# Moving four row copies ahead of V's second half in the first body, with a total and two signs later

## What is computed

```python
Q = (h @ Wq.T + bq)          # h = layernorm(x); 16 heads of 32; V likewise
latent = latent_keys.reshape(64, 16, 32)
logits = einsum('bhtd,lhd->bhtl', Q, latent) / sqrt(32)
w, idx = softmax of the 4 largest logits of each row
attn = (sum of w * latent[idx] + V) @ Wo.T + bo
x = x + layernorm(attn)
wu, wg, wd = ternary(W_up), ternary(W_gate), ternary(W_down)
    # scale = mean(|W|) + 1e-8; clip(round(W / scale), -1, 1) * scale
hidden = silu(layernorm(x) @ wu.T) * (layernorm(x) @ wg.T)   # 2048 wide
x = x + layernorm(hidden @ wd.T)
```

## Time and profile before

| what | value |
|---|---|
| median of 3 runs | 1028.66 us (1027.9 to 1029.03) |
| time of the profiled execution | 1029.43 us |
| its span | 1027.6 us |
| mean granted TensorE clock | 0.984 of full speed |
| PE busy | 966.2 us, 94% of the span |
| DVE, ACT, POOL busy | 71%, 50%, 52% |

### The profile page before, as it was taken

The page is one execution under the profiler, slowest core; times in us unless marked ns, Lnnn a source line. Parts: engine busy times, 40 slices in busy tenths (PEclk is TensorE's granted clock), DMA queues, the critical chain, the costliest instruction groups (busy, mean ns, idle before and its releaser), DMA issues.

```text
span 1027.6 us, 17907 instructions
## 1 busy us (share of the span) xinstructions
PE 966.2 (94%) x5738; PEld 469.4 (46%) x5738; DVE 729.3 (71%) x2666; ACT 513.9 (50%) x801; POOL 533.6 (52%) x451
## 2 busy tenths in 40 slices
PE   3738999999999999999999999999999999999997
PEld 2413544345444544445444454445444454445443
DVE  7898798376893689665993779836895669845433
ACT  5787986445534555345444455345453454433430
POOL 2556266645566446554666546564565545643330
PEclk9868999999999999999999999999999999999999
DMA  9953403532124402233113321243022511212001
GB/s 296 400 108 69 149 1 83 141 73 76 22 42 109 107 11 41 62 92 93 21 34 89 75 69 21 47 116 92 11 41 62 97 37 21 42 41 63 1 1 41
DMA packets 149331, 76.91 MB, mean 75 GB/s; under 512 B 135825, under 2 KB 135825, under 8 KB 148113
## 3 DMA queue, kind: packets, MB, share of 16 engines
q1 hardware_dynamic: 149264, 76.18, 29.5%
HBM read 34.21 MB, written 8.39 MB: 41 GB/s over the span
## 4 chain that ended last, share of the span: by engine, by line
PE 68%; DVE 15%; ACT 5%; POOL 5%; issue 4%; DMA 3%; SPq 0%; DVEq 0%; ACTq 0%; POOLq 0%
PE ug L709 36%; PE ug L728 14%; PE ring L559 10%; PE ring L687 4%; PE ring L605 2%; DVE Lr L1580 2%; DMA X1T<-halves 1%; DMA x_in<-in_x 1%; DVE v L1554 1%; DVE halves L1534 1%; DVE row L1671 1%; POOL halves L1297 1%; DVE sty L1674 1%; DVE stx L1694 1%; DVE ugt L1539 1%
## 5 line engine op out<-in xcount | busy, mean ns | idle before, releaser
L709 PE MATMUL ug<-X1T,TU 128*128 128x512 f16 (+1 forms) x1152 | 245.1, 356 | 6.3 <-DVE ugt L1544 4.2
L1274 POOL TENSOR_TENSOR hT<-ugt,hT 128x512 f16<-128x512 f32 x128 | 166.8, 1303 | 161.1 <-ACT hT L1026 161.1
L709 PE MATMUL ug<-X1T,TG 128*128 128x512 f16 (+1 forms) x1152 | 244.8, 355 | 0.0
L728 PE MATMUL ug<-TD,hT 128*128 128x512 f16 x960 | 210.9, 379 | 0.9 <-ACT TD L905 0.9
L1013 ACT ACTIVATE ugt<-ug,cu 128x512 f32<-128x512 f32 x128 | 87.9, 687 | 203.1 <-PE ug L709 202.2
L709 PEld LDWEIGHTS ug<-X1T,TU 128*128 128x128 f16 x1152 | 110.0, 98 | 116.2 <-DVE ugt L1544 4.9
L709 PEld LDWEIGHTS ug<-X1T,TG 128*128 128x128 f16 x1152 | 112.7, 98 | 108.6
L1539 DVE SCALAR_TENSOR_TENSOR ugt<-ugt,ug 128x512 f32<-128x512 f32 x128 | 87.4, 683 | 99.6 <-ACT ugt L1013 98.3
L728 PEld LDWEIGHTS ug<-TD,hT 128*128 128x128 f16 x960 | 93.2, 98 | 115.8 <-issue 3.0
L1580 DVE MATCH_REPLACE8 Lr<-v,Lb 128x68 f32<-128x68 f32 x512 | 102.3, 218 | 0.0
L1544 DVE SCALAR_TENSOR_TENSOR ugt<-ugt,ug 128x512 f32<-128x512 f32 x128 | 87.9, 687 | 4.4
(11 more groups left out here) (218 smaller groups left out, 1498.5 us busy)
## 6 DMA issues: line engine op xcount, KB each, us to landing
out_dram<-Lr SPq DMA_DIRECT2D x32, 256.0 KB, 3.2
x_in<-in_x SPq DMA_DIRECT2D x7, 1024.0 KB, 5.3
x<-in_x SPq DMA_DIRECT2D x28, 256.0 KB, 3.3
PT<-in_Wd SPq DMA_DIRECT2D x8, 512.0 KB, 6.7
hT<-in_Wu SPq DMA_DIRECT2D x4, 512.0 KB, 8.7
hT<-in_Wg SPq DMA_DIRECT2D x4, 512.0 KB, 15.4
x_in<-in_Wd SPq DMA_DIRECT2D x4, 512.0 KB, 5.1
x_in<-in_x SPq DMA_DIRECT2D x4, 256.0 KB, 4.3
```

What stands on the lines that cost most here:

```text
L709: last = pe.matmul(ug[:, 2 * (e % 2) + s, cols], w[:, k, e * P:(e + 1) * P], X1T[:, b, k, cols], start=(k == 0 and b == 0), stop=(k == KD ...
L728: last = pe.matmul(down_bank(kind, t), hT[:, a, e, t * P:(t + 1) * P], td[:, e, :], start=(first and e == of[0] and a == 0), stop=(final a ...
L1274: pool.tensor_tensor(hT[:, 1, e, :], ugt[:, 2 + e % 2, :], hT[:, 0, e, :], ALU.subtract).then_inc(h_lo, 1)
```

## The change

In the first body, ACT copies all four tiles of chunk 1's rows ahead of `vw_half(m, 1)`, and sums pieces 10 and 11 behind them. POOL makes chunk 1's row factors (`ln1_rstd_of(1)`) after two of the four first-half remainders, and all four `s1_lo` ahead of the second-half remainders. DVE makes `ln1_biases(1)` and Wo's remainder (`weights_lo(2)`) ahead of the total of the first matrix and the sum of piece 14; at the end, `t2_lo(0, 3)` ahead of `round_to(1)`. PE takes the gate matrix's total after `q(0)` of the second body. On ACT, `t2_rows(-1, 3)` comes ahead of `q(1)`. In the second body's loop the signs of pieces 7 and 15 move from block 6 to blocks 8 and 9. The order of DVE's roundings stays as it was, written out as `ROUND_ORDER`.

```diff
@@ -271,14 +271,15 @@
 
         ASUM_DVE = (2, 3, 14, 15)
         ASUM_ACT = (0, 1, 16, 17, 18, 19) + tuple(range(4, 14)) + tuple(range(20, 24))
-        TERN_ORDER = (0, 8, 1, 9, 4, 12, 2, 10, 5, 13, 3, 11, 6, 14, 7, 15, 22, 23, 16, 17, 20, 21, 18, 19)
+        TERN_ORDER = (0, 8, 1, 9, 4, 12, 2, 10, 5, 13, 3, 11, 6, 14, 22, 7, 15, 23, 16, 17, 20, 21, 18, 19)
 
         ROUND_ACT = (18, 19)
         ROUND_POOL = (0,)
+        ROUND_ORDER = (8, 1, 9, 4, 12, 2, 10, 5, 13, 3, 11, 6, 14, 7, 15, 22, 23, 16, 17, 20, 21)
 
         def rounded_before(n):
 
-            return sum(q not in ROUND_POOL for q in TERN_ORDER[:TERN_ORDER.index(n) + 1])
+            return ROUND_ORDER.index(n) + 1
 
         def after_tern(*pieces):
 
@@ -755,12 +756,13 @@
                     wo(2)
                     pe.wait_ge(tern_step, 1)
                     wo(3)
-                    wait(pe, a32_ready, i, KD, KD)
-                    total(weight_sum(1), tot[:, 1:2], tot_ready, 2, tota_ready)
                     return
                 if att:
                     for m in range(KD):
                         q(m)
+                        if kind == "second" and m == 0:
+                            wait(pe, a32_ready, j, KD, KD)
+                            total(weight_sum(1), tot[:, 1:2], tot_ready, 2, tota_ready)
                 logits_after = (8, 12) if kind == "second" else (6, 10)
                 for half in range(2):
                     upgate(0, half)
@@ -1080,16 +1082,16 @@
                     probs_hi(3)
                     vw_half(2, 0)
                     vw_half(3, 0)
-                    abs_sum(10)
-                    abs_sum(11)
                     s1_rows(1, 0)
                     s1_rows(1, 1)
+                    s1_rows(1, 2)
+                    s1_rows(1, 3)
                     vw_half(0, 1)
                     vw_half(1, 1)
                     vw_half(2, 1)
                     vw_half(3, 1)
-                    s1_rows(1, 2)
-                    s1_rows(1, 3)
+                    abs_sum(10)
+                    abs_sum(11)
                     abs_sum(12)
                     abs_sum(13)
                     t2_rows(0, 0)
@@ -1100,8 +1102,8 @@
                 if kind == "second":
                     q(0)
                     t2_rows(-1, 2)
+                    t2_rows(-1, 3)
                     q(1)
-                    t2_rows(-1, 3)
                     sign(1)
                     sign(9)
                     q(2)
@@ -1115,7 +1117,7 @@
                         if m < 2:
                             t2_rows(-1, 2 + m)
                 late = kind == "second"
-                SIGN_AT = {0: (2,), 1: (10,), 2: (5, 13), 3: (3, 11), 4: (6,), 5: (14,), 6: (7, 15), 8: (22,), 9: (23,), 10: (16,), 11: (17,), 12: (20,), 13: (21,)}
+                SIGN_AT = {0: (2,), 1: (10,), 2: (5, 13), 3: (3, 11), 4: (6,), 5: (14,), 8: (22, 7), 9: (15, 23), 10: (16,), 11: (17,), 12: (20,), 13: (21,)}
                 SUM_AT = {2: (4,), 3: (5,), 4: (6, 7)}
                 exp4_at = (4, 7, 12) if late else (3, 6, 11, 15)
                 exps_at = (6, 10, 15) if late else (5, 9, 13)
@@ -1318,17 +1320,17 @@
                     shift(3)
                     normalise(2)
                     normalise(3)
-                    for m in range(KD):
-                        low_a_half(m, 0)
+                    low_a_half(0, 0)
+                    low_a_half(1, 0)
                     ln1_rstd_of(1)
-                    s1_lo(1, 0)
-                    s1_lo(1, 1)
+                    low_a_half(2, 0)
+                    low_a_half(3, 0)
+                    for t in range(TT):
+                        s1_lo(1, t)
                     for m in range(KD):
                         low_a_half(m, 1)
                     rstd_y(0)
                     rstd_y(1)
-                    s1_lo(1, 2)
-                    s1_lo(1, 3)
                     rstd_x(0, 0)
                     rstd_y(2)
                     round_to(0)
@@ -1764,10 +1766,10 @@
                     probs_lo(2)
                     ln1_stat(1)
                     probs_lo(3)
+                    ln1_biases(1)
+                    weights_lo(2)
                     tern_total(0)
                     abs_sum(14)
-                    ln1_biases(1)
-                    weights_lo(2)
                     abs_sum(15)
                     y_a(0)
                     y_a(1)
@@ -1788,8 +1790,8 @@
                     y_b(3)
                     t2_lo(0, 2)
                     y_c(0, 3)
+                    t2_lo(0, 3)
                     round_to(1)
-                    t2_lo(0, 3)
                     round_to(9)
                     round_to(4)
                     round_to(12)
```

## The result

The changed kernel takes 1031.37 us (median of 10 runs, 1029.33 to 1032.67) against 1029.05 for the kernel before (10 runs beside it). The ratio is 1.0020, 95% interval 1.0011 to 1.0028: 1.1 to 2.9 us slower, best estimate 2.1. I had forecast 0.6 us faster.

A forecast was written before the change was run, and what follows sets the result against it. PE, busy 94% of the span, was taken to set the time after the opening; ACT's queue, then DVE's, orders blocks 0 to 7. A 0.6 gain at the first tanh carries through: 1028.66 - 0.6 = 1028.06, say 1028.0; range 1025.9 to 1029.8.

The forecast's parts named there:

- The gap of PE: PE between wo(3) and q(0): earlier rows fill XT sooner, so q ends at 97.5 instead of 104.08, 6.6 us sooner.
- The second idle stretch before X1T: PE after q: idles 2.8 us from 97.5, possibly at low clock for the first half blocks, which still end by about 107.
- DVE: DVE before y_a(0): factor about 1.2 sooner gains up to 1.0; 0.2 (0 to 0.5) taken for the y_a, y_b, y_c chain.
- What the rows push back: V's second half on ACT, its POOL remainders and wo(2) slightly later; 0.1 taken for wo(3), between 0 and 0.5.
- The end of the opening: ACT from t2_rows(-1, 3) to the first tanh: tanh at 109.75 in place of 110.34, a gain of 0.6.
- The 0.45 for the fourth rows: ACT's t2_rows(-1, 3) ahead of q(1): can begin at about 100.1 instead of 100.54, 0.45 sooner.
- The signs and the port: Second body's loop: moved signs cost nothing, with 0.15 to spare; DVE roundings meeting POOL taken as nothing, from -1.2 to +1.0.
- rival B: ACT in block 10: sign 15 delays the tanh beyond its cover, +1.04 and +0.2 against -0.6; 1029.3, chance 0.15.
- The prediction's term for the rounding at 151: DVE rounding beside POOL's probs_lo: 1.2 less if it goes first, 1.0 more if it waits; nothing taken.
- rival A: Port meeting falls well (-1.2) and PE's further waits shrink by up to 1.1, about -2.9 in all; 1025.8, chance 0.18.
- Rival C: PE's idling from 97.5 keeps half clock through all four half blocks, block 2 ending 2.1 later; 1030.8, chance 0.06.

The follow-up runs named there:

- e1: Kernel before with only POOL's row factor moved between the second and third of the four first-half remainders; ratio 1.0013 to the kernel before.
- e2: Changed kernel with POOL's row factor back behind all four first-half remainders; ratio 1.0017 to the kernel before.
- e10: Kernel before with POOL's row factor ahead of all four first-half remainders; ratio 1.0023 to the kernel before.
- e6: Changed kernel with DVE's total and sum of piece 14 back ahead of ln1_biases(1) and Wo's remainder; ratio 1.0017 to the kernel before.
- e15: Changed kernel with only the extra PE matmuls of e9 in both gaps, before and inside wo_first(0); ratio 1.0016 to the kernel before.
- e9: Kernel before with the factor early as in e1, ten unused PE matmuls before wo_first(0) and nine inside it; ratio 0.9996 to the kernel before.
- e13: Changed kernel with e6's edit and the extra PE matmuls of e9 in both gaps; ratio 1.0011 to the kernel before.
- e5: Kernel before with only t2_rows(-1, 3) ahead of q(1) on ACT and t2_lo(0, 3) ahead of round_to(1) on DVE; ratio 1.0002 to the kernel before.
- e4: Kernel before with only the signs of pieces 7 and 15 moved from block 6 to blocks 8 and 9; ratio 1.0005 to the kernel before.
- e7: e1 with ten extra matmuls on PE, product unread, between weigh_half(0) and wo_first(0); ratio 1.0006 to the kernel before.

## Why the prediction was wrong

**The gap of PE: right.** q ran from 88.6 to 99.2 at full clock, 1.5 later than forecast against the weigh half, since `wo(3)` ended late; XT was full in time, the total behind `q(0)` cost 0.14. (In the text, "4.7 of them the gap less the total" is the gap alone; less the total it is 4.4, and with the clock's 2.2 that is the 6.6.) The second idle stretch before X1T was there (2.96 at 102.20, I had said 2.8) and brought the low clock back for the first half blocks (0.60 granted on average from 102.2 to 106), covered by the transfer of tiles 2 and 3, as I had written. None of it reached the sum, as forecast.

**DVE: this is the step that failed.** I wrote that the factor "comes about 1.2 sooner, so DVE gains up to 1.0", and took 0.2 of gain. Against the weigh half the factor did come 1.2 sooner, but partly by luck: the power instruction started 2.2 sooner, met DVE's subtraction and took 1.0 more [e1; not in e2 or e10]. And `y_a(0)` came 1.72 later. The sum is -1.24 for the factor, +0.46 for the biases, +1.39 for Wo's remainder and +1.11 for the sum of piece 14 with its total. Two of these were in no part of the step. The sum of piece 14 had filled all but 1.00 of DVE's wait for the factor and was moved behind it, so it now lies on the path: e6 takes it back and gains 0.8 in `y_a(0)`. And Wo's remainder takes 5.02 instead of 3.64. It is four instructions, of 0.74 each where POOL is quiet. Before and in e2 only the fourth met a row subtraction of POOL and took 1.66 and 1.64; POOL's rows began 1.7 to 1.8 after Wo's remainder did in all three kernels, so their start alone is not the cause. In the changed kernel the early factor lets Wo's remainder start while POOL still has the delayed remainders of V; the first instruction takes 1.23 for that, so the third has not begun when POOL's rows do, and the third and the fourth take 1.64 each. It takes both moves: with the factor alone (e1) the rows begin 2.6 after it and it is 3.22, with the rows but the factor back (e2) it is 3.63. e15 shows that DVE's path alone holds `y_a(0)` at 16.3.

**What the rows push back: mis-sized.** I took 0.1 "between 0 and 0.5" for V's late second half. V's second remainders began at 81.81 where I had 80.2, since ACT's rows began at 74.79 and not at 73.19. The prediction contradicts itself there: it starts the rows at 73.19 and has the factor, which they need, only 1.2 sooner than 75.1. The term in front of `wo(2)`, the delay of the first-half remainders by the factor, I had not priced at all: 1.31 us of wait, and 3.4 us more at the low clock (71.6 to 79.0, for 71.35 to 75.3 before). It costs 1.04 in `y_a(0)` alone (e1), and by way of the clock: at full clock the same late remainder leaves `y_a(0)` at 14.31 (e9). In the changed kernel it is covered by DVE's longer path (e15). With both mended (e13), `y_a(0)` is still 0.6 late and the first tanh 1.2: DVE's slower remainder of Wo, and V's late second half by way of `wo(2)` and POOL's factor of y.

**The end of the opening: wrong, small.** The 0.45 for the fourth rows did not come. Measured from `y_c(0, 3)`, the first tanh is 10.39 behind it after and 10.30 before; in e5 it is 10.38. The rows start 0.26 sooner where I had 0.45, and the waits for roundings are 0.67 (0.27 and 0.40) where I had put 0.2 for both; together these are 0.7, the distance from the 0.6 forecast to the 0.09 lost. ACT's work in between, 9.5, was as forecast.

**The signs and the port: small gains.** From the first tanh to V it is 57.25 before, 56.79 after; e4 has 57.05 and e5 57.00, so the two edits give 0.2 and 0.25, and together they are the 0.45. Block 10's tanh cost nothing, so rival B did not occur. The prediction's term for the rounding at 151, from -1.2 to +1.0, came out on the good side (0.88 for 1.94 in the trace after), as did part of rival A, but little of it arrived: PE still waited for `hidden` on DVE, 0.16 at 161.59 for 0.36 at 159.99 before. My working of the 1.94 there does not quite add up either: 0.75 behind the rest of POOL's 2.13 is 2.14. Rival C's low clock occurred without its price.

**Sum.** +1.72 at `y_a(0)`, +1.80 at the first tanh, -0.45 to V: +1.34. The page "SBUF — State Buffer" of the Trainium skill, section "SBUF: two separate sides", gives the rule that I set against the rounding at 151 only. It would have asked the question where it mattered, at the factor's new place: a subtraction with two inputs from SBUF was then due on DVE. The traces agree in part. POOL waited for DVE in e1 and in the changed kernel, and each slow instruction of Wo's remainder ended 0.54 to 0.55 after the POOL subtraction that it met (before, the changed kernel, e1, e2, e10); but in e10 DVE was not held by POOL's power instruction.

## What to carry to other kernels

An instruction moved earlier lands beside other work: look up what each neighbouring engine does in the very microsecond of the new place, and price the same instruction beside that work, not at its old duration. Before a step is moved out of a wait that it fills, count it as new work on the path. And where PE's short waits keep it near the low clock, look at what a wait does to the clock behind it: here a remainder 1.0 us late put `y_a(0)` 1.0 later at half clock (e1) and left it 0.3 sooner than before at full clock (e9). The 19 matmuls whose product nobody reads, with the factor early, brought the opening 1.1 us forward, more than any reordering here; without the early factor they were not tried, and the whole time of e9 does not show a gain.

## What the runs showed of the hardware that I had not expected

The power instruction on POOL (4 numbers a partition) took 2.04 when a DVE subtraction of 1024 columns had begun 0.09 earlier (changed kernel, e1), and 1.05 when it began 0.34 before that subtraction (e10), which itself kept its 1.23 either way. An instruction of Wo's remainder on DVE (128x512) that starts while POOL is in a subtraction ends 0.54 to 0.55 after POOL's does, and so takes 1.15 to 1.66 instead of 0.74 (before, changed kernel, e1, e2, e10). One idle stretch of 2.03 us on PE was followed by matmuls at twice the distance (e7, from 73.27, granted clock 0.50 from 73 to 76), though those before it had run at full clock, while the four half blocks of the trace before went on at full clock over 0.61.
